# Layer 2 of a graph kernel: the destination rows are added by the gather's own transfers instead of by TensorE

## The chip, the cores and the metric

The program runs on one core of a Trainium2 chip. Its time is the device time of that core in microseconds, from one launch that computes the whole network (four layers). The number reported is the median of several executions. Beside it there is one profiled execution, from which every duration below is taken.

## The reference

3125 nodes with 64 features and 100,000 edges that are sorted by destination go through four pre-norm graph layers with residuals. The change is in the third one, called layer 2, in which x is the layer's normalised input, start and end are the edges' two nodes, D is 64 and H is 128:

```python
xs = x[start]
edge_inputs = jnp.concatenate([xs, x[end]], axis=1)
h = jax.nn.relu(edge_inputs @ We1 + be1)
e = jax.nn.sigmoid(h @ We2 + be2)
m = e * xs
m_sum = jax.ops.segment_sum(m, end, num_segments=n)
m_max = jax.ops.segment_max(m, end, num_segments=n)
messages = jnp.concatenate([m_max, m_sum], axis=-1)
node_inputs = jnp.concatenate([messages, x], axis=1)
x_out = jax.nn.relu(node_inputs @ Wn1 + bn1) @ Wn2 + bn2 + x
```

The product with We1 splits into a part of the source node and a part of the destination node, so both are computed once a node, and an edge only has to add two rows of 128 numbers.

## The kernel before, in words

**Layout.** Partition p holds 784 consecutive edges, as 784 columns; 8 columns (K) are a group of 1024 edges, and there are 98 groups (NG). Layer 2 has a node phase, then an edge phase that goes over the 98 groups, then a node phase. A table tab2 in DRAM has a row of 192 numbers for every node: 128 of the source's part of the hidden layer and the 64 features of xs (the message words). The destination's part of the hidden layer lies in put2, in DRAM, which has a row of 128 for each edge; only the first edge of a destination's run holds its row, the others are zero.

**A group g of the edge phase, before.** Its tiles are g2 (what was gathered, 192 wide), z2 (rows of put2, 128 wide), pr2, e2, m2 (messages) and st2 (running sum and running maximum). g2 and z2 have four slots, and group g uses slot g % 4.

- SP loads the group's source numbers into `ring` (`ring_load`, L553), then its z2 rows from put2 (`load_group`, L630), and then clears the same columns of put3, which layer 3 needs (`clear_columns`, L488, 1040 KB a group).
- GpSimd (POOL) issues 8 indirect transfers (`gather2`, `gather`, L715); each fetches 128 rows of tab2 into one column of g2.
- VectorE (DVE) spreads each destination's row over its run, column by column (`fill`, L1786): z2[k] = z2[k-1] * ns + z2[k], where ns is 1 inside a run.
- TensorE (PE) adds the two parts with the identity as weights: for each half of the group a product of g2's 128 columns and one of z2's go into the same PSUM bank (`add_up`, L1357 and L1358).
- VectorE takes the relu times we2 from PSUM (`relu2`, L2152), sums over the 128 (`reduce2`, L2159).
- ScalarE (ACT) takes the sigmoid (L1042) and scales the 8 columns of message words into m2 (L1045); it also writes the running sums of an earlier group to DRAM (`keep2`, L1034).
- VectorE adds and maximises the messages along each run (`sum2`, L2173 and L2177), 8 columns each.

**What sets the order.** Each engine runs its own program over the groups. `quads` writes out six groups and then loops over four at a time (and can leave `apart` groups to be written out behind the loop). VectorE's body of group g (`edges2`) has the 8 fills of g; `relu2` of g-2 after the second fill; `reduce2` of g-2 after the fourth; and the 8 pairs of `sum2` of g-3 between them. Semaphores tie the engines: `loaded` (z2 has landed), `got` (the gather has landed), `filled2` (fills done, one by one), `summed2` (groups that PE has added), `work2`, `gate2`, `made2` (groups whose messages are made), `scan2`, `states_out`. GpSimd gathers into a slot when PE has added and ScalarE has read the group that was there:

```python
ready((ring_in[s], (uses[0] + past("2", s)) * 16 + 16),
      *(((summed2, g - 3), (made2, g - 3)) if not isinstance(g, int) or g >= 4 else ()))
gather("2", tab2, g2, M_SRC, s)
```

and SP loads z2 of group g when `filled2` has reached (g-3)*K+1 and `summed2` g-3.

Of the kernel before, what the change touches and what calls it, by code (L numbers as in the profile page):

```python
# [21 lines left out]
ALU = mybir.AluOpType  # L22
# [6 lines left out]
P = 128  # L29
# [5 lines left out]
K = 8  # L35
# [118 lines left out]
def gnn_program(nc, x, src, dst, etype, adj_v, deg_v, w0, b0, deg_coeff, coeff_param, scale_param,  # L154
# [3 lines left out]
    with ExitStack() as ctx:  # L158
# [237 lines left out]
        filled2, summed2, work2, gate2, made2, scan2 = (sem(n) for n in ("filled2", "summed2", "work2", "gate2", "made2", "scan2"))  # L396
# [111 lines left out]
        def _(sp):  # L508
# [112 lines left out]
            def load_group(n, put_rows, rows, filled_to, summed, g, s, uses):  # L621

                again = not isinstance(g, int) or g >= 4
                ring_load(n, g, s, *(((got[s], (uses[0] + past(n, s)) * 16 * K),) if again else ()))
                if again:
                    sp.wait_ge(filled_to, (g - 3) * K + 1)
                    sp.wait_ge(summed, g - 3)
                    if n == "3a":
                        sp.wait_ge(work3, (g - 4) * STEPS3 + READS3)
                sp.dma_start(rows[:, s, :, :], group_rows(put_rows, g)).then_inc(loaded[s], 16)  # L630
            def load2(g, s, uses):
                load_group("2", put2, z2, filled2, summed2, g, s, uses)
                clear_columns(sp, put3, g * K, K, 2, zero3_out)
# [16 lines left out]
            quads(sp, lambda g, s, uses: load_group("3a", put3, z3, filled3, summed3, g, s, uses))  # L650
# [16 lines left out]
        def _(pool):  # L667
# [44 lines left out]
            def gather(n, table, rows, word, h):  # L712

                for k in range(K):
                    pool.indirect_dma_start(out=rows[:, h, k, :], out_offset=None, in_=table[:, :],  # L715
                                            in_offset=bass.IndirectOffsetOnAxis(ap=ring[:, h, word + k:word + k + 1], axis=0)
                                            ).then_inc(got[h], 16)

# [80 lines left out]
            def gather2(g, s, uses):  # L799

                ready((ring_in[s], (uses[0] + past("2", s)) * 16 + 16),
                      *(((summed2, g - 3), (made2, g - 3)) if not isinstance(g, int) or g >= 4 else ()))
                gather("2", tab2, g2, M_SRC, s)
            quads(pool, gather2)
# [33 lines left out]
        def _(act):  # L838
# [196 lines left out]

            def gate(g, s, uses):
# [10 lines left out]
            quads(act, gate)  # L1047
# [66 lines left out]
        def _(pe):  # L1114
# [245 lines left out]
            quads(pe, lambda g, s, uses: add_up("2", (g2, z2), 2, 4, HID, g, s, uses, filled2, K, work2, 2, 1, summed2))  # L1360
# [114 lines left out]
        def _(dve):  # L1475
# [671 lines left out]
            def relu2(g, h):  # L2147

                beats2.group(g)
                beats2.wait()  # L2150
                dve.wait_ge(summed2, g + 1)
                beats2.add(dve.scalar_tensor_tensor(out=pr2, in0=bank(2 * h, 2).rearrange("p (k c) -> p k c", c=HID), scalar=0.0,  # L2152
                                                    in1=spread(row["we2"].unsqueeze(1), P, K, HID), op0=ALU.max, op1=ALU.mult))
# [27 lines left out]
            def edges2(g, s, uses):  # L2181

                dve.wait_ge(loaded[s], uses[0] * 16 + 16 * (1 + after("2", s)))
                for k in range(K):
                    fill(fills2, z2, hold2, g, s, k)
                    if late(g, 2) and k == 1:
                        relu2(g - 2, s % 2)
                    if late(g, 2) and k == 3:
                        reduce2(g - 2, s % 2)
                    if late(g, 3):  # L2190
                        sum2(g - 3, (s - 3) % 4, before_of(g, s, uses, 3), k)
            quads(dve, edges2)
            for g in range(NG - 3, NG):
                if g > NG - 3:
                    relu2(g, g % 2)
# [233 lines left out]
```

## Time and profile before

| | |
|---|---|
| median of 3 executions | 5005.94 us (5001.85 to 5008.78) |
| profiled execution: its span | 7674.3 us, 62690 instructions; no other time is given for it |
| mean granted TensorE clock in it | 0.652 of full speed |
| busy in it: DVE, POOL, PE, ACT | 3909.1, 3533.6, 2780.9, 1037.0 us |
| edge phase of layer 2 in it | about 4212 to 5620 us from the start |
| bytes moved | 1039.68 MB |

The profile page gives the busy time of each engine, the transfers by queue (q0 is GpSimd's, q1 SP's, q10 ScalarE's), and groups of instructions by source line, with the idle time of their engine before them and what ended it. The span of the profiled execution is 1.53 times the median, so a duration read from it isn't simply a duration of the timed runs; how the two are brought together is part of the prediction. A transfer's row on GpSimd shows the issue alone and not the transfer of the data.

### The profile page before, as it was taken

The page shows a single profiled execution, that of the slowest core. Times are in us where ns is not written, and L with a number is a line of the kernel's source. Part 1 is how long each engine was busy: PE and PEld are TensorE (multiplying, and loading weights), DVE is VectorE, ACT ScalarE, POOL GpSimd, SP SyncE. Part 2 cuts the span into 40 slices and gives each one's busy share as a digit, 9 for nine tenths or more (in the row PEclk, how much of TensorE's full clock was granted, in tenths as well). Part 3 has the DMA queues.
Part 4 walks back from the last instruction along what each step waited for, and adds up shares of the span by engine and source line. Part 5 has one row for each costly group of instructions (what it writes and reads, how often), then busy time and mean ns, then how long its engine had stood idle before and what let it go on. Part 6 is the DMA issues. An engine that isn't in the chain of part 4 may idle for free.

```text
span 7674.3 us, 62690 instructions
## 1 busy us (share of the span) xinstructions
PE 2780.9 (36%) x10695; PEld 1383.0 (18%) x10695; DVE 3909.1 (51%) x10509; ACT 1037.0 (14%) x2413; POOL 3533.6 (46%) x3645
## 2 busy tenths in 40 slices
PE   2116200156600000390003333333345556555695
PEld 1114100012300000280001111111122222222232
DVE  4127200499700000399765555555545666666995
ACT  0000000012100000280352111111120000000232
POOL 5650577300177777400003555555536566654463
PEclk5555555567755555695556666676667877777897
DMA  8100000046321111000342665565627777776593
GB/s 310 44 22 13 10 1 0 0 180 235 133 67 48 47 47 47 22 0 0 113 149 71 223 205 200 198 201 197 207 99 242 246 244 244 245 246 206 209 332 116
DMA packets 458408, 1039.68 MB, mean 135 GB/s; under 512 B 129581, under 2 KB 247829, under 8 KB 428140
## 3 DMA queue, kind: packets, MB, share of 16 engines
q1 hardware_dynamic: 167594, 579.38, 21.3%
q0 software_dynamic: 131968, 217.09, 10.3%
q10 hardware_dynamic: 158658, 241.42, 8.9%
q14 instruction: 157, 1.29, 0.0%
q8 instruction: 31, 0.51, 0.0%
HBM read 559.03 MB, written 476.15 MB: 135 GB/s over the span
## 4 chain that ended last, share of the span: by engine, by line
issue 28%; DVE 27%; another core or an unknown queue 22%; PE 9%; DVEq 9%; ACT 2%; ACTq 1%; DMA 1%; POOL 0%; SPq 0%; POOLq 0%
DVE arena L1786 6%; DVEq L110 3%; PE psum L1438 2%; DVE arena L1931 2%; DVE arena L2173 2%; DVE arena L1948 2%; DVEq L1786 1%; PE psum L1133 1%; DVE arena L2177 1%; ACT arena L969 1%; PE psum L1267 1%; PE psum L1255 1%; DVE arena L1575 1%; DVE psum L1851 1%
## 5 line engine op out<-in xcount | busy, mean ns | idle before, releaser
L715 POOL DMA_INDIRECT arena<-tab,ring x2352 | 2334.4, 993 | 1397.6 <-issue 1141.6
L1357 PE MATMUL psum<-arena,ident 128*128 128x512 f32 x1176 | 746.6, 722 | 1465.6 <-DVE arena L1786 1348.6
L1786 DVE SCALAR_TENSOR_TENSOR arena<-arena,ns 128x64 f32<-128x64 f32 (+2 forms) x2351 | 871.7, 371 | 612.0 <-issue 464.0
L757 POOL DMA_INDIRECT weights<-arena x784 | 774.1, 987 | 385.1 <-issue 331.6
L1931 DVE SCALAR_TENSOR_TENSOR arena<-iota_row,base,psum 128x200 f32<-128x200 f32 x784 | 278.1, 418 | 1082.8 <-remote 672.0
L1358 PE MATMUL psum<-arena,ident 128*128 128x512 f32 x1176 | 686.9, 669 | 0.0
L1321 PE MATMUL psum<-agg,arena 128*128 128x200 bf16 x2352 | 263.1, 267 | 1047.8 <-issue 943.4
L1357 PEld LDWEIGHTS psum<-arena,ident 128*128 128x128 f32 x1176 | 252.1, 229 | 1855.2 <-issue 1341.7
L704 POOL DMA_INDIRECT put<-arena,zidx x75 | 73.5, 979 | 745.3 <-DVE arena L1899 630.4
L1321 PEld LDWEIGHTS psum<-agg,arena 128*128 128x128 bf16 x2352 | 211.4, 104 | 1085.5 <-issue 991.1
L2275 DVE SCALAR_TENSOR_TENSOR arena<-psum,rowb 128x1024 f32<-128x1024 f32 x196 | 238.9, 1219 | 312.6 <-remote 297.0
L1438 PE MATMUL psum<-arena,ident 128*128 128x512 f32 x784 | 361.8, 607 | 64.1 <-DVE arena L2346 63.7
L827 POOL TENSOR_TENSOR arena<-arena,score 128x256 f32<-128x256 f32 x294 | 232.4, 815 | 272.7 <-issue 120.2
L1575 DVE SCALAR_TENSOR_TENSOR arena<-psum,arena,upper 128x128 bf16<-128x128 f32 x784 | 227.2, 347 | 224.8 <-remote 124.1
L1358 PEld LDWEIGHTS psum<-arena,ident 128*128 128x128 f32 x1176 | 260.7, 222 | 357.3 <-issue 357.3
L1738 DVE TENSOR_TENSOR nodev<-psum,nodev 128x25 f32<-128x25 f32 x98 | 17.9, 183 | 551.2 <-remote 528.8
L2173 DVE SCALAR_TENSOR_TENSOR arena<-arena,ns 128x64 f32<-128x64 f32 x783 | 220.5, 282 | 136.0 <-issue 114.6
L732 POOL DMA_INDIRECT arena<-betas,eidx x25 | 24.9, 995 | 570.7 <-DVE score L2049 560.4
L1231 PE MATMUL psum<-arena 128*128 128x25 bf16 x784 | 38.3, 185 | 684.7 <-DVE arena L1748 586.5
L934 ACT ACTIVATE psum<-psum,own_row 128x512 f32<-128x512 f32 x196 | 129.7, 662 | 1115.0 <-issue 654.7
L2282 DVE TENSOR_REDUCE arena<-arena 128x8 f32<-128x512 f32 x392 | 264.9, 677 | 0.1
L2177 DVE SCALAR_TENSOR_TENSOR arena<-arena,neg 128x64 f32<-128x64 f32 x783 | 216.8, 277 | 89.1 <-issue 82.2
(424 smaller groups left out, 4679.9 us busy)
## 6 DMA issues: line engine op xcount, KB each, us to landing
put<-zero SPq DMA_DIRECT2D x98, 1040.0 KB
arena<-put SPq DMA_DIRECT2D x98, 1040.0 KB
spill<-arena ACTq DMA_DIRECT2D x98, 1024.0 KB
arena<-spill SPq DMA_DIRECT2D x98, 1024.0 KB
state<-arena ACTq DMA_DIRECT2D x147, 512.0 KB
weights<-zero SPq DMA_DIRECT2D x32, 1600.0 KB
arena<-weights SPq DMA_DIRECT2D x32, 1600.0 KB, 7.3
put<-zero SPq DMA_DIRECT2D x14, 3584.0 KB
```

Of the source, the lines that this page charges most:

```text
L715: pool.indirect_dma_start(out=rows[:, h, k, :], out_offset=None, in_=table[:, :], in_offset=bass.IndirectOffsetOnAxis(ap=ring[:, h, word + ...
L757: pool.indirect_dma_start(out=weights0[:, :], out_offset=bass.IndirectOffsetOnAxis(ap=words0[:, g, k:k + 1], axis=0), in_=words0f[:, g, K ...
L1321: mm = pe.matmul(bank(2 + 2 * h + k // 2)[:, k % 2 * NT * R:(k % 2 + 1) * NT * R], lhsT=picks[:, h, k, :], rhs=s_parts[:, a, :], start=(a ...
L1357: pe.matmul(place, lhsT=ident[:, :], rhs=rows_of[0][:, s, columns, 0:width], start=True, stop=False)
L1358: mm = pe.matmul(place, lhsT=ident[:, :], rhs=rows_of[1][:, s, columns, 0:width], start=False, stop=True)
L1438: mm = pe.matmul(bank(h).rearrange("p (c k) -> p k c", k=K), lhsT=ident[:, :], rhs=y3[:, h, :, head * D:(head + 1) * D], start=(head == 0) ...
L1575: marked = dve.scalar_tensor_tensor(out=alike[:, h * 4 + k, :], in0=bank(h)[:, k * P:(k + 1) * P], scalar=key[:, column], in1=upper[:, :], ...
L1786: beats.add(dve.scalar_tensor_tensor(out=rows[:, s, k, :], in0=before, scalar=mark(ns, g, k), in1=rows[:, s, k, :], op0=ALU.mult, op1=ALU. ...
L1931: pick = dve.scalar_tensor_tensor(out=sifted[:, h * 4 + k, :], in0=iota_row[:, :], scalar=src_column[:, column], in1=bank(2 + 2 * h + k // ...
L2173: scans2.add(dve.scalar_tensor_tensor(out=st2[:, h, k, 0:D], in0=zero[:, 0:D] if start else prior[:, 0:D], scalar=mark(ns, g, k), in1=m2[: ...
L2177: scans2.add(dve.scalar_tensor_tensor(out=st2[:, h, k, D:2 * D], in0=lowest[:, :] if start else prior[:, D:2 * D], scalar=mark(neg, g, k), ...
L2282: beats3.add(dve.tensor_reduce(rs3[:, columns, :], pr3[:, columns, :].rearrange("p k (h c) -> p k h c", c=D), AX.X, ALU.add))
```

## The change

1. VectorE's fill writes the destination's row into the group's slot of g2 (columns 0 to 127 of the 192) and not back into z2 (`fill2`); what it carries over from the column before it is also in g2.
2. ScalarE sets the 64 message words of a slot to zero (`blank`), four times ahead of the loop and then for each group right after the messages of the group in that slot are made. It waits for these first.
3. GpSimd's 8 transfers of a group add what they fetch to what is in the slot (`gather_add`): the hidden part comes on top of the filled row, the message words on top of zeros. They wait for the blank and for `filled2` to reach g*K+K+1, all fills of g and the first of g+1, since that one reads g's last column before anything is added to it.
4. TensorE's products of layer 2 are gone, and with them `summed2`. `relu2` waits for `got` and reads g2; we2 is copied to PSUM once, for its other operand.
5. SP loads z2 of group g when all fills of group g-4 are done; it waits for nothing else but the ring.

```diff
-            def load_group(n, put_rows, rows, filled_to, summed, g, s, uses):
+            def load_group(n, put_rows, rows, g, s, uses, *free):
                 again = not isinstance(g, int) or g >= 4
                 ring_load(n, g, s, *(((got[s], (uses[0] + past(n, s)) * 16 * K),) if again else ()))
                 if again:
-                    sp.wait_ge(filled_to, (g - 3) * K + 1)
-                    sp.wait_ge(summed, g - 3)
-                    if n == "3a":
-                        sp.wait_ge(work3, (g - 4) * STEPS3 + READS3)
+                    for semaphore, value in free:
+                        sp.wait_ge(semaphore, value)
                 sp.dma_start(rows[:, s, :, :], group_rows(put_rows, g)).then_inc(loaded[s], 16)
             def load2(g, s, uses):
-                load_group("2", put2, z2, filled2, summed2, g, s, uses)
+                load_group("2", put2, z2, g, s, uses, (filled2, (g - 3) * K))
...
+            def gather_add(n, table, rows, word, h):
+                for k in range(K):
+                    pool.indirect_dma_start(out=rows[:, h, k, :], out_offset=None, in_=table[:, :],
+                                            in_offset=bass.IndirectOffsetOnAxis(ap=ring[:, h, word + k:word + k + 1], axis=0),
+                                            compute_op=ALU.add).then_inc(got[h], 16)
...
             def gather2(g, s, uses):
-                ready((ring_in[s], (uses[0] + past("2", s)) * 16 + 16),
-                      *(((summed2, g - 3), (made2, g - 3)) if not isinstance(g, int) or g >= 4 else ()))
-                gather("2", tab2, g2, M_SRC, s)
-            quads(pool, gather2)
+                ready((ring_in[s], (uses[0] + past("2", s)) * 16 + 16), (blank2, g + 1),
+                      (filled2, g * K + K + (0 if isinstance(g, int) and g == NG - 1 else 1)))
+                gather_add("2", tab2, g2, M_SRC, s)
+            quads(pool, gather2, apart=4)
...
+            def blank(s):
+                act.activation(g2[:, s, :, HID:W2], zero[:, 0:K * D].rearrange("p (k c) -> p k c", c=D), ACT.Copy).then_inc(blank2, 1)
...
                 message.then_inc(made2, 1)
-            quads(act, gate)
+                if not last1(g):
+                    act.wait_ge(made2, g + 1)
+                    blank(s)
+            act.wait_ge(hold_in, 16 * (PIECES + 2))
+            for s in range(4):
+                blank(s)
+            quads(act, gate, apart=4)
...
-            quads(pe, lambda g, s, uses: add_up("2", (g2, z2), 2, 4, HID, g, s, uses, filled2, K, work2, 2, 1, summed2))
...
-            def relu2(g, h):
+            we2_up = bank(2)[:, 0:HID]
+            step(dve.tensor_copy(we2_up, row["we2"]))
+
+            def fill2(g, s, k):
+                if k == 0:
+                    fills2.group(g)
+                fills2.wait()
+                before = g2[:, s, k - 1, 0:HID] if k else hold2 if isinstance(g, int) and g == 0 else g2[:, (s - 1) % 4, K - 1, 0:HID]
+                fills2.add(dve.scalar_tensor_tensor(out=g2[:, s, k, 0:HID], in0=before, scalar=mark(ns, g, k), in1=z2[:, s, k, :],
+                                                    op0=ALU.mult, op1=ALU.add))
+
+            def relu2(g, s, use):
                 beats2.group(g)
                 beats2.wait()
-                dve.wait_ge(summed2, g + 1)
-                beats2.add(dve.scalar_tensor_tensor(out=pr2, in0=bank(2 * h, 2).rearrange("p (k c) -> p k c", c=HID), scalar=0.0,
-                                                    in1=spread(row["we2"].unsqueeze(1), P, K, HID), op0=ALU.max, op1=ALU.mult))
+                dve.wait_ge(got[s], (use + past("2", s)) * 16 * K + 16 * K)
+                beats2.add(dve.scalar_tensor_tensor(out=pr2, in0=g2[:, s, :, 0:HID], scalar=0.0,
+                                                    in1=spread(we2_up.unsqueeze(1), P, K, HID), op0=ALU.max, op1=ALU.mult))
```

How the instructions move, at the two places that the prediction speaks of. GpSimd, in its loop over four groups, before (arena is g2, tab is tab2, ring the source numbers; ISA and REGISTER_ALU are waits and their sums in the engine's sequencer):

```order
L410 ISA [waits ring_in2]
L715 DMA arena<-tab,ring 128x192 [waits summed2,made2]
L715 DMA arena<-tab,ring 128x192 x7
L410 REGISTER_ALU [waits ring_in3]
L715 DMA arena<-tab,ring 128x192 [waits summed2,made2]
```

and now:

```order
L410 ISA [waits ring_in2]
L410 ISA [waits blank2]
L720 DMA arena<-tab,ring 128x192 [waits filled2]
L720 DMA arena<-tab,ring 128x192 x7
L410 REGISTER_ALU [waits ring_in3]
```

The gather now follows VectorE's fills (`filled2`) and ScalarE's blank, where it followed PE and ScalarE's messages of four groups earlier.

VectorE, in its loop, from the first fill of a body to the relu of the group two before it, before:

```order
L1786 SCALAR_TENSOR_TENSOR arena<-arena,ns 128x128
L110 REGISTER_ALU
L2151 REGISTER_ALU [waits work2]
L2152 SCALAR_TENSOR_TENSOR arena<-psum,rowb 128x1024 [waits summed2]
L110 REGISTER_ALU
```

and now:

```order
L2170 SCALAR_TENSOR_TENSOR arena<-arena,ns 128x128
L110 REGISTER_ALU
L2177 ISA [waits work2]
L2178 SCALAR_TENSOR_TENSOR arena<-arena,psum 128x1024 [waits got0]
L110 REGISTER_ALU
```

The number and order of VectorE's instructions stay; the relu waits for the transfers themselves (`got0`), no longer for PE.

## Rows read from the trace of the kernel before

**Rows 1.** The page's first line.

```profile
span 7674.3 us, 62690 instructions
```

**Rows 2.** Busy time in the stretches without gathers or scatters: us, PE, PEld, DVE, ACT, POOL busy (x), PEclk, DMA share, GB/s.

```profile
576.00:768.00 192.00, 123.03 (x824) 85.84 (x824) 150.40 (x984) 3.17 (x5) 0.00 (x0) 0.50 0.05 14
1440.00:2100.00 660.00, 383.86 (x1842) 150.48 (x1843) 567.22 (x759) 126.28 (x143) 26.94 (x28) 0.69 0.41 153
3200.00:4085.00 885.00, 243.50 (x2690) 214.67 (x2690) 724.16 (x2361) 432.15 (x1124) 9.48 (x10) 0.64 0.19 64
7150.00:7674.00 524.00, 393.58 (x959) 164.96 (x959) 415.02 (x731) 160.64 (x116) 258.67 (x321) 0.90 0.69 240
sum 2261.00, PE 1143.97 PEld 615.95 DVE 1856.80 ACT 722.25 POOL 295.09; mean PE 285.99 PEld 153.99 DVE 464.20 ACT 180.56 POOL 73.77
```

**Rows 3.** The same columns for the gather stages of layers 1, 2 and 3.

```profile
2130.00:3180.00 1050.00, 59.96 (x368) 49.54 (x368) 33.59 (x184) 28.96 (x46) 791.86 (x759) 0.50 0.20 47
4220.00:5600.00 1380.00, 478.81 (x758) 185.79 (x759) 741.29 (x2431) 215.67 (x837) 739.03 (x772) 0.68 0.61 204
5810.00:6960.00 1150.00, 689.48 (x1418) 289.52 (x1417) 731.18 (x1403) 0.00 (x0) 696.18 (x713) 0.80 0.74 245
```

**Rows 4.** Groups by line, 4220 to 5600 us: shapes, count, busy us, mean ns, idle before.

```profile
L715 POOL DMA_INDIRECT arena<-tab,ring x772 | 739.5, 958 | 641.6 <-issue 637.7 <-PE psum L1358 4.0
L1357 PE MATMUL psum<-arena,ident 128*128 128x512 f32 x380 | 284.3, 840 | 913.5 <-DVE arena L1786 839.6 <-issue 44.9 <-DMA arena<-tab,ring 29.0
L1358 PE MATMUL psum<-arena,ident 128*128 128x512 f32 x378 | 247.0, 742 | 0.0
L1045 ACT ACTIVATE arena<-arena 128x64 f32<-128x64 f32 x744 | 187.7, 334 | 3.0
L2152 DVE SCALAR_TENSOR_TENSOR arena<-psum,rowb 128x1024 f32<-128x1024 f32 x94 | 114.6, 1219 | 54.2 <-issue 44.8 <-PE psum L1358 7.8 <-DVE arena L1786 0.8
```

**Rows 5.** What VectorE waited for, 4220 to 5600 us: total us, times, longest.

```profile
DVE arena L1786 <- issue: 344.0, 107, 7.6
DVE arena L2173 <- issue: 110.3, 68, 3.8
DVE arena L2177 <- issue: 79.5, 67, 2.6
...
DVE arena L2152 <- PE psum L1358: 7.8, 1, 7.8
```

**Rows 6.** Transfers by queue, 4220 to 5600 us: packets, MB, share of 16 engines.

```profile
q1 hardware_dynamic: 54710, 156.45, 33.1%
q0 software_dynamic: 37004, 75.86, 18.7%
q10 hardware_dynamic: 13248, 48.24, 8.7%
```

**Rows 7.** Transfers from 4878 to 4884 us, where the queues are full.

```profile
DMA packets 881, 2.39 MB, mean 398 GB/s; under 512 B 264, under 2 KB 349, under 8 KB 880
```

**Rows 8.** Order of time, 4803 to 4812 us: start, us, engine, line, [idle before <- releaser].

```profile
4803.00 1.23 DVE L2152 SCALAR_TENSOR_TENSOR arena<-psum,rowb 128x1024 f32<-128x1024 f32 x1
...
4807.02 2.02 ACT L1045 ACTIVATE arena<-arena 128x64 f32<-128x64 f32 x8
...
4809.58 0.35 DVE L1786 SCALAR_TENSOR_TENSOR arena<-arena,ns 128x128 f32<-128x128 f32 x1
4809.81 1.00 POOL L715 DMA_INDIRECT arena<-tab,ring  x1 [10.91 <-issue]
```

**Rows 9.** Order of time at 4085 us: one indirect transfer alone, and its first reader.

```profile
4085.24 0.94 POOL L724 DMA_INDIRECT open_sum<-state,open_end  x1 [336.48 <-DMA state<-arena]
4087.66 0.22 DVE L2079 TENSOR_TENSOR open_sum<-open_sum,cin 128x64 f32<-128x64 f32 x1 [3.47 <-DMA open_sum<-state,open_end]
```

**Rows 10.** From the page: ScalarE's instruction that is nearest to the blank.

```profile
L934 ACT ACTIVATE psum<-psum,own_row 128x512 f32<-128x512 f32 x196 | 129.7, 662 | 1115.0 <-issue 654.7
```

**Rows 11.** The columns of rows 2, in the node phase behind the edge phase.

```profile
5680.00:5740.00 60.00, 38.53 (x165) 24.07 (x165) 21.16 (x55) 14.77 (x27) 20.77 (x22) 0.77 0.23 81
```

More of the change, by code:

```diff
@@ L395, in gnn_program @@
         apart1 = sem("apart1")
-        filled2, summed2, work2, gate2, made2, scan2 = (sem(n) for n in ("filled2", "summed2", "work2", "gate2", "made2", "scan2"))
+        filled2, work2, gate2, made2, scan2, blank2 = (sem(n) for n in ("filled2", "work2", "gate2", "made2", "scan2", "blank2"))
         filled3, summed3, work3, scored = (sem(n) for n in ("filled3", "summed3", "work3", "scored"))
@@ L648, in _ @@
             sp.wait_ge(tab_out, 16 * (1 + 3 * NBATCH))
-            quads(sp, lambda g, s, uses: load_group("3a", put3, z3, filled3, summed3, g, s, uses))
+            quads(sp, lambda g, s, uses: load_group("3a", put3, z3, g, s, uses, (filled3, (g - 3) * K + 1), (summed3, g - 3), (work3, (g - 4) * STEPS3 + READS3)))
             def load3c(g, s, uses):
@@ L2184, in edges2 @@
                 for k in range(K):
-                    fill(fills2, z2, hold2, g, s, k)
+                    fill2(g, s, k)
                     if late(g, 2) and k == 1:
-                        relu2(g - 2, s % 2)
+                        relu2(g - 2, (s - 2) % 4, before_of(g, s, uses, 2)[0])
                     if late(g, 2) and k == 3:
@@ L2194, in _ @@
                 if g > NG - 3:
-                    relu2(g, g % 2)
+                    relu2(g, g % 4, g // 4)
                     reduce2(g, g % 2)
```

## Prediction

> **What bounds the kernel now.** I read the stretches first. The span of the profiled execution [rows 1] is 1.53 times the median of the timed ones, 5005.94 us, so the views have to be put on one scale before anything is subtracted. In four stretches GpSimd issues few or no gathers or scatters; they last 2261 us together, and VectorE is busy for 1856.80 us of them [rows 2]. Little can shrink there. If they last as long in a timed run, the rest is 7674.3 - 2261 = 5413 us traced and 5006 - 2261 = 2745 us timed: the stretches full of indirect transfers take about 0.51 of their traced time when nobody traces.
>
> The edge phase of layer 2 is one of these. The traced stretch of 1380 us has 772 gathers, 96.5 groups of 8, so a group takes 14.3 us [rows 3]. In it VectorE is busy for 741.29 / 96.5 = 7.7 us, GpSimd for 7.7 us, PE for 5.0 us, ScalarE for 2.2 us, and the 16 DMA engines for 0.61 x 14.3 = 8.7 us. The groups by line and VectorE's waits say who waits for whom. PE's products sat idle for 913.5 us and 839.6 of these ended with a fill of VectorE [rows 4]: the gathers had landed long before. VectorE's waits for PE come to 7.8 us in the whole stage, while 344.0 + 110.3 + 79.5 + 44.8 = 579 us of its idle time have no releaser at all ("issue") [rows 4, 5]. So VectorE paces the stage, with its own work and with time in which its sequencer has nothing ready; neither PE nor the gathers do. GpSimd's idle time in turn ends with ScalarE's messages: at 4809.04 the messages of a group are made, at 4809.81 the next gather starts [rows 8]. It waits for VectorE, at second hand.
>
> What is a group's pace in a timed run? From below VectorE's own 7.7 us; the share of 0.51 gives 7.3, which VectorE's work doesn't allow. From above the median's share of the span, 0.652 x 14.3 = 9.3 us. I take the middle, 8.5 us. At that pace the transfers are no longer at leisure: a group moves 204 GB/s x 14.3 us = 2.92 MB, and where the queues are full they move 398 GB/s [rows 3, 7]; that is 7.3 us of 8.5.
>
> **The change part by part.**
>
> PE's products go: 284.3 + 247.0 = 531 us of busy time [rows 4], all of it beside VectorE, which waited 7.8 us for it. Gain taken: 0, at most 8 us. The relu takes the same 1024 elements; its two sources are still one in SBUF and one in PSUM. Nothing, at 1219 ns each [rows 4]. A loss is possible behind the stage: PE comes out of it with the lower of its two clocks (layer 1's stage, in which PE hardly works, shows a granted 0.50, this one 0.68 [rows 3]), and the 38.53 us of products in the node phase ran at 0.77 [rows 11]. At 0.50 they would take 38.53 x 0.27 / 0.50 = 21 us more; most of that phase is a chain over other engines, and before it PE stood still too, so I count 0 and keep 0 to 21 us.
>
> ScalarE's blank: 512 elements, nearest to the 662 ns of its 128x512 instruction [rows 10], 98 times. ScalarE is busy for 2.2 us of a group, eight messages of 334 ns among them [rows 4], and the blank is wanted four groups later. Its wait for `made2` holds up only the next group's write of the states and its sigmoid, by some 0.8 us, and their reader comes a body later. Nothing, with ScalarE's idle time as cover.
>
> SP's loads of z2 are free of PE and of one fill. They have three bodies of lead before and after. Nothing.
>
> GpSimd's 784 issues become adding ones. The trace shows none. From below the plain one, 958 ns [rows 4]; from above twice that, which would make 15.3 us a group in the traced scale, more than the stage's whole pace; that is a rival. I take the plain one, since the indices and rows of a transfer are the same.
>
> **The transfers** get more to do, and this is the first term. The 8 gathers of a group read 1024 rows of 768 bytes, 0.79 MB; to add, the engines must also read the same bytes of the slot. By bytes a group needs 3.71 MB / 398 GB/s = 9.3 us instead of 7.3. By engine time the gathers' queue q0 takes 18.7% of 14.3 us = 2.67 us a group [rows 6], and between nothing and once more this comes on top: 8.7 to 11.4 us in all. I take the bytes, which lie between them: 9.3 us.
>
> The Trainium skill has a rule that speaks against the change: in "Collectives: The Full Stack", section on the bandwidth ceiling, a reducing transfer is half as fast as a copying one, not because of the add but because it needs two source reads on the same ring. No row here shows an adding transfer; taken whole, the rule is the upper end of the line above, 98 x 2.67 = 262 us.
>
> **The new loop** is the second term. Before, a gather had four groups of lead. Now gather g can start only after the first fill of g+1, and the relu of g comes in the body of g+2. So: gather g's eight issues, its landing, relu of g, the rest of body g+2, the first fill of g+3, and only then gather g+2. Two groups can't take less than this sum. In timed terms an issue is 1050 / 759 = 1.38 us of layer 1's stage, which GpSimd paces [rows 3], times 0.51 = 0.70 us; seven of them are 4.9 us. The last one's landing takes 4087.66 - 4085.24 = 2.4 us alone [rows 9]; behind a group's z2 load and clear (1.55 MB, 3.9 us at 398 GB/s) 6.3 us. From the relu's start to the next body's first fill is 4809.58 - 4803.00 = 6.6 us, and 0.35 for the fill [rows 8], 0.2 for the semaphore: 7.1 us. Together 14.4 to 18.3 us for two groups, 7.2 to 9.2 for one; with the adding reads in the queue too, one more. So the loop and the transfers meet at about the same pace, and as neither has slack I put the new pace at 9.7 us, 0.4 above the transfers' floor.
>
> **The ends.** The first gather waits for nine fills, 3 us; the last one starts only after the last fill, so 4.9 + 2.4 us stand where four products of 0.8 us stood, 4 us. Together 7 us.
>
> **Sum**: (9.7 - 8.5) x 98 = 118, and 7: 125 us. 5006 + 125 = **5131 us**. For its ends: pace 9.3 against 9.3 before gives +7, pace 10.4 against 8.5 gives +193, so this case covers about 5015 to 5210.
>
> **The rivals.**
>
> *Heavy adding transfers.* GpSimd's issue costs about twice and q0's engine time doubles. For it: the rule above, and that nothing in this kernel adds this way yet. The loop becomes 7 x 1.4 + 4.4 + 7.1 = 21.3 us, 10.7 a group; with 11.4 of engine time the pace is 11.4 to 12: 98 x (11.7 - 8.5) + 7 = 321 us, 5327 us.
>
> *No change.* VectorE's 7.7 us and its own empty time set the pace before and after, and the reads of SBUF come beside the others for free. For it: 579 us of VectorE's idle time hang on nobody, and a timed pace of 9.3 leaves room for all of the above. Time 5006, within 10 us.
>
> *Faster: the gate moves forward.* Today GpSimd idles for 641.6 us because a gather hangs on the messages of four groups back, which VectorE and ScalarE finish late in a body [rows 4, 8]; that makes gathers come in bursts of two groups, and full queues hold up everybody. The new gate is the first instruction of a body. If gathers and z2 loads then flow evenly, the pace falls from 8.5-9.3 to VectorE's 7.7 plus half a microsecond. This decides if a landing stays under about 4 us, so that the loop stays under 8.2. Price: (8.2 - 9.3) x 98 = -108 us, 4898 us. Against it: VectorE, which would have to be helped, hardly waits for anything the change moves [rows 5].
>
> **How the numbers follow.** The forecast's case has 0.45, the heavy one 0.19, no change 0.12, faster 0.24. A measurement here can tell about 0.2%, 10 us. Slower by more: 0.45 + 0.19 = 0.64; same 0.12; faster 0.24. The range takes in the faster case down to a little beyond its centre and the heavy one's centre: 4885 to 5335 us. The likeliest case alone has 5015 to 5210.
>
> **What would show it.** Right: VectorE's relu (L2178) now waits with a gather named as its releaser, some us a group; q0's share per group grows above 2.67 us; the issues stay near 0.96 us; bursts of GpSimd are no longer two groups long. ScalarE has 98 blanks of about 0.66 us that nobody waits for. Wrong: the relu's wait is near zero (then no loop), q0's time per group is unchanged (then adding is free), or issues of 1.5 us and more (the heavy case). A stage shorter than 1380 us for 96.5 groups with VectorE's empty time gone would be the faster rival.

## The result, and the profile after

| | median us | executions |
|---|---|---|
| before | 5005.5 | 4 (5001.85 to 5008.78) |
| changed | 5484.41 | 4 (5481.42 to 5490.78) |

The ratio is 1.0959, with a 95% interval of 1.0944 to 1.0975: 479 us slower. The prediction had the sign, but 125 us instead of 479, and its range ended at 5335 us.

The profiled execution of the changed kernel was also timed: 5490.78 us, for a span of 5488.9 us. Here the span is the time. The trace of before that the prediction rests on [rows 1] was not of that kind. A second profiled execution of the same kernel, run 1 below, took 5011.47 us with a span of 5009.7 us, and it is the one to compare with. On some chips at some times this kernel takes about 7600 us and not 5006, and the first trace has the marks of such an execution (last section).

The changed kernel, the page's head (slices of 137 us):

```profile
span 5488.9 us, 60911 instructions
...
DVE  8867999889998654555555555554688888789993
...
POOL 6777777467777777788888888885777777734662
...
q0 software_dynamic: 207232, 217.09, 19.8%
...
POOL 49%; issue 21%; DVE 11%; PE 10%; DMA 6%; DVEq 1%; SPq 0%; ACT 0%; POOLq 0%; ACTq 0%
```

The kernel before, in its second profiled execution, the same rows (slices of 125 us):

```profile
span 5009.7 us, 62690 instructions
...
DVE  8876999978999866356777777737788788789993
...
POOL 6777777737777777767777777747777777715652
...
q0 software_dynamic: 131968, 217.09, 15.3%
...
POOL 38%; issue 19%; PE 17%; DVE 13%; DMA 10%; DVEq 1%; ACT 1%; POOLq 0%; ACTq 0%; SPq 0%
```

GpSimd's share of the chain that ended last grows from 38 to 49%, TensorE's falls from 17 to 10%, and VectorE's slices in the stage go from 7 to 5: it has the same work over a longer time. GpSimd reads 7 in nearly every slice of before up to the 35th. In the first trace it had 5s in layer 2's edge phase (slices 23 to 29), and whole gaps of 0 elsewhere:

```profile
POOL 5650577300177777400003555555536566654463
```

A 7 is not a sign of room here: the timeline shows what it is made of, an issue of 0.95 us, 0.30 us of nothing that the trace names, and the next issue.

GpSimd's timeline from 2600 us, before (second execution) and after (start, us, engine, line, idle before and releaser):

```profile
2600.57 0.95 POOL L715 DMA_INDIRECT arena<-tab,ring  x1 [0.30 <-issue]
2601.82 0.95 POOL L715 DMA_INDIRECT arena<-tab,ring  x1 [0.30 <-issue]
```

```profile
2601.35 1.55 POOL L720 DMA_INDIRECT arena<-tab,ring  x1 [0.30 <-issue]
2603.20 1.55 POOL L720 DMA_INDIRECT arena<-tab,ring  x1 [0.30 <-issue]
```

In both the issues stand back to back, with that 0.30 us between them. Now 1000 us inside layer 2's edge phase, in the columns of [rows 3]; before, then after:

```profile
2300.00:3300.00 1000.00, 440.27 (x768) 176.44 (x769) 735.50 (x2492) 222.81 (x862) 742.00 (x762) 0.73 0.80 272
```

```profile
2300.00:3300.00 1000.00, 0.00 (x0) 0.00 (x0) 508.06 (x1726) 196.29 (x666) 837.93 (x533) 0.50 0.81 194
```

GpSimd's count is the number of gathers, 533, after; in before it is 762, of which 15 belong to what follows the last gather of layer 2 at 3254.9 us. After, a group of 8 takes 8000 / 533 = 15.0 us; by the starts of its first and last gather, 2263.3 and 3737.6 us, 1474.3 x 8 / 783 = 15.06. The phase of before without its end, as a window of its own:

```profile
2260.00:3240.00 980.00, 439.42 (x766) 175.47 (x767) 724.85 (x2446) 217.96 (x846) 746.85 (x766) 0.74 0.83 285
```

That is 766 / 8 = 95.75 groups and 10.23 us each, of which GpSimd's eight issues with their 0.30 us make 8 x (0.975 + 0.30) = 10.2 us (746.85 / 766 = 0.975). No part of a group's 10.23 us is left in which GpSimd could have waited for another engine, and after the change it is the same with 8 x (1.578 + 0.30) = 15.0 us. GpSimd paces before and after; run 8 tests it for before. (15.06 - 10.23) x 98 = 473 of the 479 us arise here.

The groups of the changed kernel that answer to [rows 4, 5, 10]:

```profile
L713 POOL DMA_INDIRECT arena<-tab,ring x1568 | 1515.3, 966 | 478.1 <-issue 466.9 <-DVE arena L2308 5.5 <-DVE arena L2301 4.9
L720 POOL DMA_INDIRECT arena<-tab,ring x784 | 1237.3, 1578 | 248.6 <-issue 229.4 <-DVE arena L2170 19.2
...
L2178 DVE SCALAR_TENSOR_TENSOR arena<-arena,psum 128x1024 f32<-128x1024 f32 x98 | 119.7, 1221 | 620.2 <-DMA arena<-tab,ring 620.2
...
L1043 ACT ACTIVATE arena<-zero 128x512 f32<-128x512 f32 x98 | 61.3, 629 | 23.2 <-DMA arena<-rows,dst 20.3
```

The plain gathers of layers 1 and 3 (L713) last 966 ns as before; the adding ones (L720) last 1578 ns. VectorE's relu (L2178) waits 620.2 us for gathers, 6.3 us a group. The gate on the fills (`DVE L2170`) holds GpSimd up for 19.2 us in the whole program.

### The profile page after: what moved, and what is told of

It is laid out like the page before. It is cut to its first block, busy times and chain, and to the rows that moved or that the text cites. A ratio compares the mean times of both kernels' runs of the same rounds, so it can differ in the third digit from the quotient of the medians.

```text
span 5488.9 us, 60911 instructions
## 1 busy us (share of the span) xinstructions
PE 2257.1 (41%) x9911; PEld 1162.1 (21%) x9911; DVE 3883.0 (71%) x10510; ACT 1098.3 (20%) x2511; POOL 3944.5 (72%) x3645
## 4 chain that ended last, share of the span: by engine, by line
POOL 49%; issue 21%; DVE 11%; PE 10%; DMA 6%; DVEq 1%; SPq 0%; ACT 0%; POOLq 0%; ACTq 0%
POOL arena L713 19%; POOL arena L720 16%; POOL weights L762 13%; DMA arena<-tab,ring 4%; PE psum L1452 3%; PE psum L1372 3%; PE psum L1373 2%; DVE arena L2372 1%; DMA weights<-zero 1%; DVE arena L2081 1%; DVE arena L2199 1%; DVE arena L1800 1%; DVE arena L2170 1%; DVE arena L2203 1%; DVE arena L1962 1%
## 5 line engine op out<-in xcount | busy, mean ns | idle before, releaser
L713 POOL DMA_INDIRECT arena<-tab,ring x1568 | 1515.3, 966 | 478.1 <-issue 466.9
L720 POOL DMA_INDIRECT arena<-tab,ring x784 | 1237.3, 1578 | 248.6 <-issue 229.4
L1800 DVE SCALAR_TENSOR_TENSOR arena<-arena,ns 128x64 f32<-128x64 f32 (+1 forms) x1567 | 601.9, 384 | 208.7 <-ACT arena L974 90.3
L1372 PE MATMUL psum<-arena,ident 128*128 128x512 f32 x784 | 458.0, 669 | 254.4 <-DMA arena<-tab,ring 189.5
L2178 DVE SCALAR_TENSOR_TENSOR arena<-arena,psum 128x1024 f32<-128x1024 f32 x98 | 119.7, 1221 | 620.2 <-DMA arena<-tab,ring 620.2
L1373 PE MATMUL psum<-arena,ident 128*128 128x512 f32 x784 | 436.2, 640 | 0.0
L1452 PE MATMUL psum<-arena,ident 128*128 128x512 f32 x784 | 360.8, 606 | 64.7 <-DVE arena L2372 64.4
L2170 DVE SCALAR_TENSOR_TENSOR arena<-arena,ns 128x128 f32<-128x128 f32 x784 | 270.4, 345 | 109.2 <-issue 108.2
L1051 ACT ACTIVATE arena<-arena,par 128x8 f32<-128x8 f32 x98 | 29.5, 301 | 1191.6 <-DVE arena L2185 1191.6
L2372 DVE TENSOR_TENSOR arena<-arena,score 128x256 f32<-128x256 f32 x490 | 244.8, 538 | 26.7 <-PE psum L1452 26.4
L1372 PEld LDWEIGHTS psum<-arena,ident 128*128 128x128 f32 x784 | 156.2, 210 | 496.2 <-issue 343.9
L974 ACT ACTIVATE arena<-arena,score 128x64 f32<-128x64 f32 x784 | 197.6, 334 | 242.8 <-DVE arena L1800 121.9
L1282 PE MATMUL psum<-arena 64*128 64x400 f32 x512 | 165.9, 736 | 148.7 <-DVE arena L1874 141.0
## 6 DMA issues: line engine op xcount, KB each, us to landing
weights<-zero SPq DMA_DIRECT2D x32, 1600.0 KB, 18.3
```

What stands on the lines that cost most here:

```text
L1372: pe.matmul(place, lhsT=ident[:, :], rhs=rows_of[0][:, s, columns, 0:width], start=True, stop=False)
L1373: mm = pe.matmul(place, lhsT=ident[:, :], rhs=rows_of[1][:, s, columns, 0:width], start=False, stop=True)
L1452: mm = pe.matmul(bank(h).rearrange("p (c k) -> p k c", k=K), lhsT=ident[:, :], rhs=y3[:, h, :, head * D:(head + 1) * D], start=(head == 0) ...
L1800: beats.add(dve.scalar_tensor_tensor(out=rows[:, s, k, :], in0=before, scalar=mark(ns, g, k), in1=rows[:, s, k, :], op0=ALU.mult, op1=ALU. ...
L2170: fills2.add(dve.scalar_tensor_tensor(out=g2[:, s, k, 0:HID], in0=before, scalar=mark(ns, g, k), in1=z2[:, s, k, :], op0=ALU.mult, op1=ALU ...
L2372: makes3.add(dve.tensor_tensor(y3[:, s % 2, k, :].rearrange("p (h c) -> p h c", c=D), gc3[:, s, k, 0:HD].rearrange("p (h c) -> p h c", c=D ...
```

## The experiments

Each "before" is the kernel before, timed on the same chip beside the run. Runs 1, 4 and 9 are one execution each, run 10 is the median of two, the others of four to ten.

| run | edit | us | before | ratio, 95% |
|---|---|---|---|---|
| 1 | before, again | 5011.47 | 5007.54 | single |
| 2 | new order, plain gathers | 5122.16 | 5007.54 | 1.0228 (1.0211 to 1.0245) |
| 3 | old order, adding gathers | 5478.69 | 5007.54 | 1.0939 (1.0921 to 1.0957) |
| 4 | changed kernel, adds 64 numbers a row | 5478.41 | 5007.54 | single |
| 5 | run 2, gate split | 5022.17 | 5008.91 | 1.0027 (1.0016 to 1.0038) |
| 6 | changed kernel, gate split | 5483.83 | 5008.91 | 1.0949 (1.0931 to 1.0968) |
| 7 | old order, products gone | 5000.22 | 5008.91 | 0.9984 (0.9975 to 0.9994) |
| 8 | old order, every second gather adds | 5256.87 | 5008.91 | 1.0497 (1.0480 to 1.0515) |
| 9 | old order, adding, 64 rows | 7653.20 | 7661.45 | single |
| 10 | run 9 again | 5388.41 | 5004.19 | 1.0769 (1.0738 to 1.0801) |
| 11 | old order, plain, 64 rows | 7652.05 | 7601.90 | 1.0061 (1.0044 to 1.0078) |
| 12 | run 11 again | 7644.32 | 7590.13 | 1.0073 (1.0056 to 1.0091) |

**Run 1, the kernel before again.** No edit.

> The kernel before, unchanged, to get a second profiled execution of it. The first one had a span of 7674.3 us against timed runs of 5006 us, while the changed kernel's span (5488.9 us) is its timed one (5490.8 us). Theory A (the first profiled execution was an odd one): this span is about 5004 us, the gathers of layer 2 stand at 0.96 us and 0.30 us apart, so 10.0 us a group, and GpSimd is busy nearly without a gap in that stage: some 10.2 us a group, 1000 us in all. Theory B (what I predicted from: gathers go faster in timed runs, 0.70 us, and the stage's pace is 8.5 us): the span is again far above 5006 us.

Measured: the rows above. So the gathers last as long as in the first trace (969 ns against 958 in [rows 4]), and what is missing is the gaps between them. TensorE's products, which in [rows 4] waited for VectorE's fills, wait mostly for the gathers here, and VectorE's relu waits 121.1 us for TensorE where the first trace had 7.8 (2260 to 3240 us):

```profile
L1357 PE MATMUL psum<-arena,ident 128*128 128x512 f32 x384 | 259.0, 762 | 564.8 <-DMA arena<-tab,ring 456.6 <-DVE arena L1786 107.8 <-issue 0.3
...
L2152 DVE SCALAR_TENSOR_TENSOR arena<-psum,rowb 128x1024 f32<-128x1024 f32 x95 | 115.7, 1218 | 121.2 <-PE psum L1358 121.1
```

**Run 2, the new order with plain gathers.**

```diff
-                                            compute_op=ALU.add).then_inc(got[h], 16)
+                                            ).then_inc(got[h], 16)
```

> The changed kernel with plain transfers in place of the adding ones: all new waits, fills, blanks and the missing products stay; the destination's part isn't added and the fills are overwritten. Theory A (the adding transfer's issue on GpSimd, 1.58 against 0.96 us, is the whole loss): time back to 5006 within 20 us, issues 0.96 us. Theory C (the new loop of gather, relu and fill costs time too): 5050 to 5130 us, with the relu waiting some us for gathers while GpSimd idles. Theory D (the new order frees something): under 4990 us.

Measured: 115 us slower than before. The stage's first gather starts at 2264.0 us and its last at 3373.6: 11.3 us a group. Its gathers and its relu:

```profile
L720 POOL DMA_INDIRECT arena<-tab,ring x784 | 763.6, 974 | 357.2 <-issue 222.7 <-DVE arena L2169 134.2 <-ACT arena L1042 0.3
...
L2177 DVE SCALAR_TENSOR_TENSOR arena<-arena,psum 128x1024 f32<-128x1024 f32 x98 | 119.6, 1221 | 253.9 <-DMA arena<-tab,ring 253.0
```

With short issues the new loop is real: GpSimd waits 134.2 us for the fill that opens the gate, and VectorE 253.0 us for gathers; each waits for the other in turn.

**Run 3, adding gathers in the old order.** The kernel before, with `compute_op=ALU.add` in layer 2's gathers and nothing else (they add into what their slot held).

> The kernel before, with its layer 2 gathers made adding ones and nothing else changed; they add to what the slot held from the group before, so the values of layer 2 are meaningless. Theory A (the issue): 5006 + 784 x 0.61 = 5484 us, the same as the changed kernel within 20 us, issues 1.55 to 1.58 us. Theory C (new waits): only part of it, 5400 us or less. Theory E (the products of PE now collide with something): above 5520 us.

Measured: 471 us slower, with TensorE's products, the old gate and no blanks. The page's group of its gathers:

```profile
L722 POOL DMA_INDIRECT arena<-tab,ring x784 | 1236.5, 1577 | 239.1 <-issue 236.9 <-PE psum L1365 1.8 <-DMA ring<-meta 0.3
```

(1577 - 969) ns x 784 = 477 us. One operand of one instruction carries the loss. The other parts of the change together add 479 - 471 = 8 us to it, which is no more than the two intervals leave open.

**Run 4, adding 64 numbers a row in place of 192.** The changed kernel; each gather fetches 128 rows of 64 numbers from the same table seen as rows of 64, and adds them to the first 64 columns of the slot's rows, at the same places of the program. The values are other ones, and the message words are not gathered.

> The changed kernel with adding transfers of 64 numbers a row in place of 192 (128 rows each as before; the source is a view of the same table in rows of 64, so other data). Theory A1 (the cost of an adding issue is per row): issues stay at 1.55 us and the time at 5484 us. Theory A2 (the issue is slow because the queues push back, or goes by bytes): issues fall towards 1 us or by a third, and the time goes down by 150 us or more.

Measured: 5478.41 us, within 6 us of the changed kernel, with a third of the bytes on the adding queue. Transfers by queue in the stage, 2300 to 3300 us; changed kernel, then this run:

```profile
DMA packets 123608, 194.35 MB, mean 194 GB/s; under 512 B 21230, under 2 KB 89443, under 8 KB 123526
...
q0 software_dynamic: 76739, 52.42, 39.0%
```

```profile
DMA packets 123626, 158.81 MB, mean 159 GB/s; under 512 B 89612, under 2 KB 89612, under 8 KB 123543
...
q0 software_dynamic: 76780, 17.51, 20.2%
```

Its issues, of the same length as the changed kernel's (a median of 1550 ns there too):

```profile
L720 POOL DMA_INDIRECT arena<-tab,ring x784: 1541/1550/1728, 2261.1 to 3729.7; - x196
```

The share of q0 falls from 39.0 to 20.2%, the packets stay, the issues and the time stay. So neither the bytes nor the DMA engines behind the queue set the pace, and the issue isn't long because the engines are behind.

**Run 5, run 2 with the gate split.** The first four gathers of a group wait for its fifth fill, the other four as before (the helper takes the columns as an argument).

```diff
-                      (filled2, g * K + K + (0 if isinstance(g, int) and g == NG - 1 else 1)))
-                gather_add("2", tab2, g2, M_SRC, s)
+                      (filled2, g * K + 5))
+                gather_add("2", tab2, g2, M_SRC, s, range(0, 4))
+                ready((filled2, g * K + K + (0 if isinstance(g, int) and g == NG - 1 else 1)))
+                gather_add("2", tab2, g2, M_SRC, s, range(4, K))
```

> The new order with plain gathers, and GpSimd's gate cut in two: the first four gathers of a group start after its fifth fill, the other four after the first fill of the next group. (Layer 2's rows are gathered without being added.) The whole gate cost 115 us with plain gathers, 11.3 us a group against 10.2. Theory (it is the loop through VectorE's body: the fills of a whole body lie ahead of the first gather): half a body less in the loop of two groups, so GpSimd's own 10 us a group binds again and the time is 5000 to 5035 us, with the relu's wait for gathers well below its 253 us. Rival (not the loop, but the fills writing where gathers write, or VectorE's wait for a gather at the relu as such): 5110 to 5130 us, as with the whole gate.

Measured: 5022.17 us, 13 us over before. 101 of the 115 us are gone, and the waits that formed the loop shrink with them:

```profile
L720 POOL DMA_INDIRECT arena<-tab,ring x784 | 761.9, 972 | 256.9 <-issue 216.5 <-DVE arena L2171 40.3
...
L2179 DVE SCALAR_TENSOR_TENSOR arena<-arena,psum 128x1024 f32<-128x1024 f32 x98 | 119.6, 1220 | 155.2 <-DMA arena<-tab,ring 155.2
```

What cost the time was the gate's place: a whole body of fills ahead of a group's first gather.

**Run 6, the changed kernel with the gate split.** The same edit, gathers adding.

> The change with the same cut gate and its adding gathers. Theory (the issue of an adding gather, 1.58 us with 0.30 us to the next, paces the stage at 15 us a group, and the loop is hidden under it): no more than 10 us from the change, 5470 to 5490 us. Rival (issue and loop add up, and the loss is shared by both): the 115 us of the loop come back, about 5370 us.

Measured: 5483.83 us, against 5484.41. Where an issue takes 1.58 us the loop lies under GpSimd's own work and moving the gate gains nothing that can be told from noise; the two losses don't add up.

**Run 7, the products alone gone.** The kernel before without TensorE's products of layer 2. The relu reads the gathered rows and waits for `got`; the destination rows are left out of the sum. With `summed2` gone, GpSimd's gate waits for the relu of four groups back in its place, SP's loads wait for the fill alone, and we2 is read from PSUM as in the changed kernel.

```diff
-            quads(pe, lambda g, s, uses: add_up("2", (g2, z2), 2, 4, HID, g, s, uses, filled2, K, work2, 2, 1, summed2))
...
-                      *(((summed2, g - 3), (made2, g - 3)) if not isinstance(g, int) or g >= 4 else ()))
+                      *(((work2, (g - 4) * 2 + 1), (made2, g - 3)) if not isinstance(g, int) or g >= 4 else ()))
```

> The kernel before without TensorE's products of layer 2, the gate on the messages of four groups back kept, gathers plain; the relu takes the gathered rows alone, so that the destination's rows are left out of the sum. Theory (the stage is paced by GpSimd's issues at 10 of 10.2 us a group; TensorE is on nobody's path): within 10 us of the kernel before, 5000 to 5015 us. Rivals: TensorE's chain between fills, relu and gathers was in the pace, then up to 40 us faster; or the relu's direct wait for gathers, which has no TensorE between, costs, then up to 50 us slower.

Measured: 5000.22 us, 8.7 us faster (0.06 to 0.25% by the interval). In the old order, taking TensorE's work away wins this much and no more.

**Run 8, every second gather adds.** The old order; `compute_op=ALU.add` for even `k` in layer 2 (the sums are of other rows).

> The kernel before, with every second gather of layer 2 adding into what its slot held (the sum is of other rows then). All of them adding cost 471 us. Theory (the price sits on each adding issue, 0.61 us on GpSimd): half of it, 392 x 0.61 = 239 us, 5235 to 5255 us, with two kinds of issue in one group, about 0.97 and 1.58 us. Rival (the price is the queue backing up when the engines fall behind, which needs a run of adding transfers): less than 100 us, or durations between the two kinds.

Measured: 248 us slower, 53% of run 3's loss for half of its adding gathers. GpSimd's timeline in the stage:

```profile
2600.31 1.56 POOL L716 DMA_INDIRECT arena<-tab,ring  x1 [0.30 <-issue]
2602.18 1.09 POOL L716 DMA_INDIRECT arena<-tab,ring  x1 [0.31 <-issue]
2603.57 1.55 POOL L716 DMA_INDIRECT arena<-tab,ring  x1 [0.30 <-issue]
2605.43 0.98 POOL L716 DMA_INDIRECT arena<-tab,ring  x1 [0.30 <-issue]
```

Long and short alternate one by one: the price belongs to the instruction, not to a state of the queue. That the loss is already there for half of them, in full proportion, also says that GpSimd had no slack in the kernel before.

**Runs 9 and 10, adding over 64 partitions.** Run 3, with `rows[0:64]` and `ring[0:64]` in layer 2's gathers (half of the rows left out).

> The kernel before with adding gathers in layer 2, each over 64 partitions in place of 128 (the other half of the rows is left out). Theory (the added time is per row, since each row became a packet of its own, 96 packets more a gather): the issue falls by much more than a tenth, to about 1.1 to 1.3 us, and the time to about 5100 to 5250 us. Rival (a fixed price of the adding form per instruction): the issue stays at 1.5 us or more and the time near 5470 us.

> The same kernel as the last, for a time beside an ordinary execution of the kernel before: the last one's went with an execution of the kernel before of 7661 us. In its trace all gathers together had a mean of 1169 ns, which leaves (2352 x 1169 - 1568 x 966) / 784 = 1575 ns for an adding one of 64 rows, as long as with 128. If the price is per instruction, the time is that of adding with all rows, 5460 to 5490 us, with a GpSimd that issues back to back. If it is per row and the last trace only hid it, the time is about 5100 to 5250 us.

Measured: run 9 was executed where the kernel before took 7661.45 us, so its time can't be set beside 5006. It shows something else: its 784 adding gathers stand back to back from 4231.4 to 5614.6 us, 1383 us, and the plain ones of the first trace took as long, 1395 us, with gaps. Where an execution leaves GpSimd idle, the dearer issue fills the gaps. Run 10 took 5388.41 us, 384 us over before, which is between the two expectations, nearer to the one per instruction. The rows of its gathers and one of its issues:

```profile
L717 POOL DMA_INDIRECT arena<-tab,ring x2352 | 2656.6, 1130 | 717.2 <-issue 701.7 <-DVE arena L2277 6.7 <-DVE arena L2284 4.6
```

```profile
2600.03 1.42 POOL L717 DMA_INDIRECT arena<-tab,ring  x1 [0.30 <-issue]
```

An adding issue is (2656.6 - 1568 x 0.966) / 784 = 1.457 us over 64 rows, 1.577 over 128. I had taken 1.575 us from run 9's mean over all gathers, in which the plain ones were not at 966 ns; its adding ones alone have a mean of 1.462 us. If the line through the two is straight, a row costs 1.9 ns and the rest, 1.34 us, comes with each adding instruction, more than a whole plain gather. This is an estimate from two points. The packets fall with the rows, from 144 a gather to 45363 / 568 = 80 (run 10, 2300 to 3300 us), and the issue gets only 0.12 of its extra 0.61 us shorter.

**Runs 11 and 12, plain over 64 partitions.** The kernel before with layer 2's gathers over half of the rows, not adding.

> The kernel before with layer 2's gathers, plain, over 64 partitions in place of 128 (half of the rows is left out). With adding, 64 rows took 1.457 us on GpSimd and 128 rows 1.577, so 1.9 ns a row. Theory (GpSimd's issues pace the stage, and a plain issue has the same slope): 0.85 us an issue, so 784 x 0.12 = 94 us faster, 4905 to 4925 us. If the slope belongs to the adding form alone, the issue stays at 0.95 to 0.97 us and the time within 10 us of the kernel before. Rival (VectorE paces the stage, as the prediction had it): the issue gets shorter and the time stays within 10 us of the kernel before.

> The same kernel as the last, whose comparison ran where the kernel before takes 7602 us. In its trace a plain issue over 64 rows lasts 0.90 us, against 0.95 over 128: 0.05 to 0.07 us less on each of 784. Theory (GpSimd's issues pace the stage where the kernel before takes 5006 us): 40 to 55 us faster than the kernel before, 4950 to 4970 us. Rival (VectorE paces it, as the prediction had it): within 10 us of the kernel before.

Both were executed where the kernel before takes 7600 us, and there the kernel was 0.6 to 0.7% slower, not faster; why slower stays open. The issues did get shorter (a median of 903 ns in run 11 against 946 in the first trace, both in layer 2's edge phase), so in such executions GpSimd's issues don't pace the stage; whether 784 times 0.05 us would have shown at 5006 us stays open.

No version beat both kernels in a way that computes the reference: run 7's 9 us leave out the sum that the products were for.

## Why the prediction was wrong

Three steps failed. The third, the plain price for an adding issue, carries the number; the first two hid that GpSimd had no room for a dearer one.

**The scale, the first step, failed, and with it most sizes.** The step was that the gather stretches take "about 0.51 of their traced time when nobody traces". A duration was never the thing to scale: a plain gather is 958 ns in the first trace, 969 in the second, 966 after. Rows at hand spoke against it. GpSimd is busy for 3533.6 us in the first trace and for 295.09 of them in the four stretches [rows 2]; the other 3239 us of work had to fit into the 2745 us that the step left for them. They can't. The execution of 5010 us does it by having gathers run beside layer 1's VectorE work, which the first trace kept apart [rows 2, 3]; us, PE, PEld, DVE, ACT, POOL busy of run 1:

```profile
1150.00:2230.00 1080.00, 336.28 (x3331) 281.30 (x3331) 827.03 (x2697) 477.88 (x1200) 810.51 (x850) 0.66 0.38 110
```

Busy times over the timed run would have helped, if read with the gaps between issues. By busy time alone VectorE leads, 3909.1 of 5006 us, 78%, against GpSimd's 3533.6, 71%. But the first trace has the 0.30 us too:

```profile
4811.12 0.95 POOL L715 DMA_INDIRECT arena<-tab,ring  x1 [0.30 <-issue]
```

With that behind each of the 3136 gathers and scatters GpSimd is at 89%, and a group of layer 2 can't take less than 8 x (0.958 + 0.30) = 10.1 us, above the 8.5 us that the prediction took.

**"VectorE paces the stage" failed.** What paced the stage in the first trace stays open: VectorE was busy for 741.29 of its 1380 us [rows 3]. In executions of 5006 us the pace is 10.23 us a group and GpSimd fills it; VectorE has 724.85 / 95.75 = 7.6 us of work. Run 8's proportional loss confirms it. The timed pace of 8.5 us was too short by 1.7.

**The plain price for an adding issue failed.** I wrote 958 ns, "since the indices and rows of a transfer are the same", and put twice that into a rival. Measured: 1578 ns, 1.63 times. That alone is (1.578 - 0.969) x 784 = 477 us. The rival of heavy adding transfers (0.19) had the price, an issue about twice as long and q0's engine time doubled, and its sign, "issues of 1.5 us and more", is the one that came. It still had the pace from the loop and the engine time. Its 5327 us was short because it too scaled the issues, to 1.4 us for each with its gap; measured 1.88. Eight of those are 15.04 us a group, and (15.04 - 10.23) x 98 = 471 us is nearly the whole result.

**The transfers' term was mis-sized and doesn't bind.** In the changed kernel q0 takes 0.390 x 15.0 = 5.9 us of the 16 engines per group; in the second trace of before (2260 to 3240 us) 0.254 x 10.23 = 2.6 us:

```profile
q0 software_dynamic: 36873, 75.58, 25.4%
```

The upper end, once more the plain time, was 5.3. All queues together are at 0.81 x 15.0 = 12.2 us a group, not the 9.3 by bytes, and still under GpSimd's 15.0; run 4 takes (39.0% - 20.2%) x 15.0 = 2.8 us of it away and gains nothing. The rule that the prediction weighed, in the Trainium skill's "Collectives: The Full Stack", the section on the bandwidth ceiling (there for the reducing step of a collective: half as fast, for its second source read), is near the engine time here, 5.9 / 2.6 = 2.3 times; but the adding gather also has three times the packets, and the runs don't tell the two causes apart. As a rule on the kernel's time it points to the wrong resource. The Trainium skill calls descriptor generation "small, variable" within the fixed cost of one transfer ("DMA: Bandwidth & Descriptors", anatomy of a transfer on GpSimd's path). For a stream of gathers it can't be read as small: the whole issue, which the trace doesn't split, is 0.97 us a gather and 1.58 us an adding one, on the engine that sets the time.

**The loop was right in kind and short in size.** The prediction had 7.2 to 9.2 us a group; run 2 has 11.3. With issues at 0.95 + 0.30 in place of 0.70 its own sum reads 7 x 1.25 + (2.4 to 6.3) + 7.1 = 18.3 to 22.2 us for two groups, 9.1 to 11.1 for one. (The 0.2 us for a semaphore in its 7.1 stands in none of its rows; run 2 has 0.13 us from a fill's end at 2621.39 us to the gather it releases at 2621.52.) It is hidden in the changed kernel (run 6), so this term adds nothing to the result. The likeliest case's upper end has a slip: 5006 + 193 is 5199, not 5210.

**Right, in part by luck:** TensorE's products gain 0, "at most 8 us" (8.7 in run 7). The reason given, that VectorE waits 7.8 us for them, doesn't hold in executions of 5006 us, where it waits 121.1 us; nothing comes of that because GpSimd sets the pace. The blank lasts 629 ns, under the 662 of [rows 10], and its trace names nobody who waits for it. The 7 us for the ends were not measured by themselves: new order, ends and all else together are the 8 us of run 3, within noise. The sign to look for, the relu waiting for gathers, came, but as a consequence of slow issues and not as the proof of the loop that the prediction would have read in it: run 3 has the same wait, through TensorE, in the old order.

## What to carry to other kernels

Before reading who waits for whom, hold a trace's span against the timed median. Where they differ by half, as here, the durations of instructions can stand while the waits don't, and each engine's instructions, with the smallest gap that is seen between them, bound the timed run without any scale. An engine that reads 7 tenths busy with small instructions can be full. And adding in a gather wasn't free work on idle DMA engines: it was paid at the engine that issues, mostly per instruction. Such a change is worth trying only where that engine has room.

## What the hardware showed that was not expected

**An adding gather.** 1.58 us on GpSimd against 0.97, with 192 or 64 numbers a row, and 1.46 us with half the rows. It has a packet for each row: 76739 / 533 = 144 packets a gather, against 36873 / 766 = 48 for a plain one in the second trace of before. In run 10, with 64 rows, it is 80. So there is one for each row and 16 more. What in an adding issue takes the extra time, no run here shows.

**The same kernel at 5010 and at 7674 us.** Rows of VectorE's L1738, a small sum that runs 98 times in a loop, in the first and in the second profiled execution of before:

```profile
L1738 DVE TENSOR_TENSOR nodev<-psum,nodev x98: 172/184/198, 864.0 to 1564.6; 128x25 f32<-128x25 f32 x98
its engine sat idle before it (us, times) until:
  remote: 528.8, 26
  issue: 20.8, 1
```

```profile
L1738 DVE TENSOR_TENSOR nodev<-psum,nodev x98: 176/176/184, 473.7 to 617.7; 128x25 f32<-128x25 f32 x98
its engine sat idle before it (us, times) until:
  PE psum L1231: 0.5, 1
```

In the first the loop takes 701 us in place of 144, and 550 of them are 27 stops of 20 us, which no release in the trace explains. The timeline has them one after another, 22 us apart:

```profile
1016.84 0.18 DVE L1738 TENSOR_TENSOR nodev<-psum,nodev 128x25 f32<-128x25 f32 x1 [20.84 <-remote]
...
1039.29 0.18 DVE L1738 TENSOR_TENSOR nodev<-psum,nodev 128x25 f32<-128x25 f32 x1 [20.70 <-remote]
```

The instruction itself lasts as usual (a median of 184 ns against 176). The traces of runs 9, 11 and 12 have 27 such stops at the same instruction too. The longer time went with chip and hour and not with the kernel: before took 7661 us once, then 7602 and 7590 us as medians of seven, on three chips, one of which had given the 5008.91 us of runs 5 to 8. What it is was not found out; no run here shows it.
